# Writing small TensorE operations in the column tiling of the matmuls around them, in a fused audio tower of attention and routed experts

## What is computed

```python
h = _L0_tok_ref(x)                                   # interpolation, 64-point spectra, soft minimum
h = h + _L0_attn_ref(_layernorm(h, axis=-1), ...)    # sigmoid(q k^T * 8) v Wo, relu
h = h + _L0_ffn_ref(_layernorm(h, axis=-1), ...)

# inside the feed-forward layer
all_out = _experts_mlp(x, eW1, eb1, eW2, eb2, eW3, eb3)   # 64 -> 128 -> 64 -> 64, four experts
shared = _shared_mlp(x, sW1, sb1, sW2, sb2, sW3, sb3)     # 64 -> 64 -> 128 -> 64
gates = jax.nn.softmax(x @ gW + gb, axis=-1)
topv, topi = jax.lax.top_k(gates, 2)
topw = jax.nn.softmax(topv, axis=-1)
```

## Time and profile before

| | |
|---|---|
| median of 3 runs | 159.5 us (158.09 to 161.44) |
| the profiled execution | 159.61 us |
| its span, first to last instruction | 157.8 us |
| mean granted TensorE clock | 0.978 |
| TensorE matmul busy | 146.2 us, 93% of the span |
| ScalarE busy | 119.1 us, 75% |
| VectorE busy | 110.8 us, 70% |
| GpSimd busy | 55.3 us, 35% |

### The profile page before, as it was taken

The page is one execution under the profiler, slowest core; times in us unless marked ns, Lnnn a source line. Parts: engine busy times, 40 slices in busy tenths (PEclk is TensorE's granted clock), DMA queues, the critical chain, the costliest instruction groups (busy, mean ns, idle before and its releaser), DMA issues.

```text
span 157.8 us, 6710 instructions
## 1 busy us (share of the span) xinstructions
PE 146.2 (93%) x2856; PEld 87.5 (55%) x2856; DVE 110.8 (70%) x281; ACT 119.1 (75%) x163; POOL 55.3 (35%) x102
## 2 busy tenths in 40 slices
PE   7999686999997999999999999999999999999980
PEld 2478432544574666666665656443657567476480
DVE  2497998998877558586863154879488987877760
ACT  3698982887977899999997989779647867758510
POOL 7000019697695834737356225457000000000000
PEclk9999857999999999999999999999999999999999
DMA  4390000276696692777989700110001011010112
GB/s 118 102 258 1 4 0 0 67 181 145 197 255 206 201 229 72 210 215 224 165 250 179 149 4 13 25 37 0 6 4 32 5 36 34 5 32 13 30 35 67
DMA packets 16722, 15.02 MB, mean 95 GB/s; under 512 B 4780, under 2 KB 15952, under 8 KB 16628
## 3 DMA queue, kind: packets, MB, share of 16 engines
q1 hardware_dynamic: 15924, 13.99, 35.0%
q10 hardware_dynamic: 768, 0.59, 1.3%
HBM read 9.06 MB, written 4.60 MB: 87 GB/s over the span
## 4 chain that ended last, share of the span: by engine, by line
PE 75%; ACT 7%; DVE 7%; POOL 4%; issue 2%; DMA 2%; DVEq 0%; POOLq 0%
PE ps L503 16%; PE ps L485 16%; PE ps L616 9%; PE ps L632 9%; PE ps L514 5%; PE ps L674 4%; PE ps L642 3%; PE ps L696 2%; PE ps L717 2%; DMA area<-x_in 2%; PE ps L540 2%; ACT area L1244 2%; PE ps L444 2%; PE ps L476 1%; ACT square L1242 1%
## 5 line engine op out<-in xcount | busy, mean ns | idle before, releaser
L1309 ACT ACTIVATE probs<-ps 125x1000 f32<-125x1000 f32 x64 | 63.0, 1005 | 8.4 <-PE ps L485 4.1
L503 PE MATMUL ps<-probs,xn 124*32 124x250 f32 (+1 forms) x512 | 40.2, 375 | 0.3 <-ACT probs L1309 0.3
L485 PE MATMUL ps<-YS,XT 128*32 128x500 f16 x448 | 35.9, 375 | 1.0 <-issue 1.0
L1327 ACT ACTIVATE area<-ps,wf 128x500 f32<-128x500 f32 x32 | 21.1, 672 | 7.7 <-PE ps L616 7.7
L936 DVE COPY ZS<-ps 128x250 f32<-128x250 f32 x32 | 13.2, 414 | 17.7 <-PE ps L503 17.7
L503 PEld LDWEIGHTS ps<-probs,xn 124*32 124x32 f32 (+1 forms) x512 | 16.4, 109 | 12.0 <-ACT probs L1309 1.4
L1341 ACT ACTIVATE area<-ps,wf 128x500 f32<-128x500 f32 x20 | 13.5, 676 | 4.7 <-PE ps L642 2.4
L632 PE MATMUL ps<-area,wf 128*64 128x500 f32 x64 | 16.3, 584 | 0.0
L514 PEld LDWEIGHTS ps<-outW,ZS 128*32 128x32 f32 (+1 forms) x512 | 11.7, 108 | 4.8 <-issue 0.9
L485 PEld LDWEIGHTS ps<-YS,XT 128*32 128x32 f16 x448 | 11.2, 96 | 5.6 <-issue 1.7
L514 PE MATMUL ps<-outW,ZS 128*32 128x64 f32 (+1 forms) x512 | 13.1, 219 | 0.2 <-issue 0.2
(11 more groups left out here) (170 smaller groups left out, 260.8 us busy)
## 6 DMA issues: line engine op xcount, KB each, us to landing
YS<-y_stage SPq DMA_DIRECT2D x28, 250.0 KB, 4.1
y_stage<-YP SPq DMA_DIRECT2D x10, 250.0 KB, 3.7
tower_out<-res SPq DMA_DIRECT2D x7, 124.0 KB
wf<-wf_in SPq DMA_DIRECT2D x1, 648.0 KB, 5.8
y_stage<-YP SPq DMA_DIRECT2D x5, 125.0 KB, 3.9
wa<-wa_in SPq DMA_DIRECT2D x1, 512.0 KB, 5.0
y_stage<-YP ACTq DMA_DIRECT2D x3, 125.0 KB, 3.0
ch<-ch_in SPq DMA_DIRECT2D x1, 160.0 KB, 4.8
```

The source lines that it names most:

```text
L485: last = mm(ps[k0:k1, 2 * (n % 2) + j, 0:TG].rearrange("p (h n) -> p h n", h=2), XT[:, g % 3, (2 * bb + cj) * P + k0:(2 * bb + cj) * P + k ...
L503: last = mm(ps[R * hh:R * hh + R, 4 + bb, half * TB:(half + 1) * TB], xn[0:keys, 4 * g + 2 * bb + cj, :], probs[0:keys, n % 3, hh, :], sta ...
L1309: fn(probs[:, n % 3].rearrange("p (j h) n -> p j (h n)", j=2), ps[0:P, 2 * (n % 2):2 * (n % 2) + 2, 0:TG], ACT.Sigmoid, scale=SCORE_SCALE) ...
L1327: fn(H1[:, g % 2, e, :], ps[:, n % 3, 0:TG], ACT.Relu, bias=wf[:, WF["b1"][0] + e:WF["b1"][0] + e + 1]).then_inc(l1_act, 1)
```

## The change

Four operations of TensorE are cut along their output partitions, so that each instruction takes as many columns of the array as the matmuls before and behind it; the first router's logits are spread over more steps, and VectorE reads them later.

- `gates(0, ...)`: each row's matmul becomes four (32, 32, 32 and 29 tokens); two rows instead of four per call, and eight calls instead of four, behind steps 48, 49, 50, 55, 56, 57, 60 and 63.
- `gates(1, ...)`: each row's matmul becomes two (64 and 61 tokens).
- `x2_transpose(7)`: two transpositions of 64 columns per tile instead of four of 32.
- `routing_T(r)`: two transpositions (64 and 8 columns) per row pair instead of one of 72.
- `gate_logits(0)` of VectorE moves behind `add_attention(6)`, `centre2(6)` and `z_take(7, 2)`. Its wait, for as many increments as `GATE_STEPS` has entries, becomes one for eight.

```diff
-GATE_STEPS = tuple(8 * (NG - 2) + t for t in (0, 1, 2, 7))
+GATE_STEPS = tuple(8 * (NG - 2) + t for t in (0, 1, 2, 7, 8, 9, 12, 15))
...
                 for i in range(4):
-                    for c in range(4):
-                        last = nc.tensor.transpose(xt[R * c:R * c + R, i, 0:P], x2s[0:P, g % 2, i, R * c:R * c + R],
+                    for c in range(2):
+                        last = nc.tensor.transpose(xt[F * c:F * c + F, i, 0:P], x2s[0:P, g % 2, i, F * c:F * c + F],
                                                    ident16[0:P, 0:P])
...
                 for i in range(rows.start, rows.stop):
-                    row = NB * r + i
-                    last = mm(ps[0:P, bank, 2 * i * E:2 * (i + 1) * E],
-                              X2T[:, row // 4, row % 4, 0:P],
-                              wg[:].rearrange("p k e -> p (k e)"), start=True, stop=True)
+                    row, wide = NB * r + i, F if r else R
+                    for q0 in range(0, P, wide):
+                        q1 = min(q0 + wide, P)
+                        last = mm(ps[q0:q1, bank, 2 * i * E:2 * (i + 1) * E],
+                                  X2T[:, row // 4, row % 4, q0:q1],
+                                  wg[:].rearrange("p k e -> p (k e)"), start=True, stop=True)
...
                 for b in range(8):
-                    last = nc.tensor.transpose(wt[:, b, 0:P], w16[:, 8 * r + b, :], ident16[0:P, 0:P])
+                    for k0, k1 in ((0, F), (F, KV)):
+                        last = nc.tensor.transpose(wt[k0:k1, b, 0:P], w16[:, 8 * r + b, k0:k1], ident16[0:P, 0:P])
...
-                    gates(0, slice(4 * i, 4 * i + 4))
+                    gates(0, slice(2 * i, 2 * i + 2))
...
                 if g == NG - 1:
-                    gate_logits(0)
                     add_attention(g - 1)
                     centre2(g - 1)
                 z_take(g, 2)
+                if g == NG - 1:
+                    gate_logits(0)
```

## The result

The changed kernel is slower: a median of 161.51 us (six runs, 159.36 to 163.19) against 158.28 us (six runs of the kernel before, 157.9 to 161.44). The ratio is 1.0168, with a 95% interval of 1.0107 to 1.0229; it is formed from the fast executions of either kernel alone, so it lies under the quotient of the two medians. The forecast was 157.2 us, with a range that ended at 159.0. Both the direction and the size were wrong.

What follows compares the result with a forecast made beforehand. TensorE was taken as the bound in nearly every step, down to about 0.90 us. 1.73 - 0.49 + 0.58 + 0.22 + 0.22 = 2.26 us saved, giving 157.2 us on the median of 159.5; range 155.6 to 159.0.

Steps and rivals of the forecast that it cites:

- old logits pieces removed from attention: Attention steps 48 to 50 give up 1.29 us and step 55 0.44 us: 1.73 us saved.
- new ones, seven on the path: Attention: eight narrow matmuls per call, 0.07 us a call, seven calls on the path: 0.49 us added, between 0.21 and 0.78.
- second logits: From line 632 to `layer1`: 1.13 us go, 32 matmuls on 64 columns take 0.55; saved 0.58, between 0.18 and 0.66.
- last token transposition: Line 524 ahead of `layer1`: two gaps of 0.11 us vanish, the four rounds stay; 0.22 us saved.
- routing transposition, r = 1: Line 554, second call: pair of 64 and 8 columns still takes eight rounds, both outer gaps go; 0.22 us saved.
- routing transposition, r = 0: Line 554, first call: both neighbours use 64*64, so the gaps stay; nothing saved.
- VectorE's order: Later `gate_logits(0)` moves the copy behind it to about 100.7, its reader at 101.79; slack 0.6 us, no cost.
- instruction stalls: Rival: 72 more matmuls and as many loads, most between 81 and 99 us, bring another "issue" stall; 158.2 us, chance 0.15.
- dear small matmul: Rival: each of 88 narrow logits matmuls costs 0.058 us, turning point 0.038; 1.8 us slower, 161.3 us; chance 0.04.
- a floor at 0.026: Rival: the 88 logits matmuls' pace has a floor of 0.026 us; saving 1.0 us, 158.5 us; chance 0.08.
- the gaps don't come from the width: Rival: gaps around TensorE's pieces come with the change of operands and all stay; no change, 159.4 us; chance 0.06.
- one more like the larger: Stall rival's size: one further "issue" stall like the 0.98 us at 49.93; saving 1.3 us, 158.2 us; chance 0.15.

Runs made afterwards that it cites:

- the order experiment: Changed kernel with each `routing_T` call's sixteen transpositions reordered, the eight of 64 columns first, then the eight of 8: 158.1 us, ratio 0.9933 to the kernel before.

## Why the prediction was wrong

Step by step, by the profiled executions:

| Step | forecast | measured |
|---|---|---|
| old logits pieces removed from attention | -1.73 | -1.73 (none is left; the size is that read before) |
| new ones, seven on the path | +0.49 | +0.3 (0.04 to 0.05 each) |
| second logits | -0.58 | -0.63 |
| last token transposition | -0.22 | -0.22 |
| routing transposition, r = 1 | -0.22 | +1.88 (2.77 against 0.89) |
| routing transposition, r = 0 | 0 | +2.00 (2.56 against 0.56) |
| VectorE's order | 0 | 0 |
| instruction stalls | a rival | +0.6 on average, not clear of chance |
| sum | -2.26 | +1.6, with the stalls +2.2 |

The ratio of 1.0168 on 158.28 us is 2.7 us (1.7 to 3.6): the sum without the stalls lies just under this interval, the sum with them inside. Between the two profiled executions the sum closes: their spans differ by 159.7 - 157.8 = 1.9 us, and their stalls in attention by 1.7 - 1.5 = 0.2, which leaves 1.7 for the 1.6 of the other rows.

**The step that failed** (term missed: 2.10 + 2.00 = 4.1 us) is the one on the routing weights: "The new pair (64 and 8 columns) lies in different column halves, so again eight rounds: saved 0.22." It asked whether the two pieces lie on different columns, and not whether they have the same tile width. The gap of 0.10 to 0.11 us had been read correctly, and taken as the reason for which the change would help; it was then counted only at the edges of each piece and never inside the one piece that mixes two widths. Fifteen inner gaps and the lost overlap in each of two calls, less one outer gap that the second no longer has, are 3.9 us. The bound "If the halves didn't overlap it would be 16 rounds and 0.25 lost" was too low for the same reason: sixteen rounds with a gap each are 2.56 us, not 0.88. With the step right, the same sum gives -2.26 + 0.22 + 1.88 + 2.00 = +1.84 us, 161.3 on the median of 159.5 and outside the recorded range on the side where the result lies.

The Trainium skill, TensorEngine Tiling (Array Packing), section Tiling Modes, states the rule: a change of tiling mode, not just of tile, drains TensorE. The traces agree, with 0.102 to 0.105 us for a change of width and about as much for a change of rows, and none between tiles of one shape.

**What was right.** The gap comes with a change of width and vanishes with it: lines 524 and 542 have none at their edges now. That it stays where both neighbours use 64*64 was forecast too, without the reason: there it is the rows that change. Narrow matmuls are cheap: 0.016 us each on 64 columns (0.50 / 32; 0.017 forecast), and some 0.005 each on 32 (0.04 / 8). The rivals of the dear small matmul (turning point 0.038) and of a floor at 0.026 fall with that. The Trainium skill, TensorEngine Tiling (Array Packing), section Performance Considerations, has an overhead of some 60 cycles for each matmul. As the pace of the whole engine, 0.025 us by the prediction's estimate, the traces contradict it for tiled matmuls; for a single tile they don't settle it, since two halves side by side take 0.031 us and four quarters add 0.02. The rival by which the gaps don't come from the width falls with the order experiment. The last instruction of `gate_logits(0)` starts at 100.09, and the copy behind it lasts from 100.23 to 100.64, in time for the projection at 101.11; the order cost nothing.

**Half right.** The stall rival named "one more like the larger" for 0.15. In the profiled execution of after it is there (1.08 us), and on average kernels with narrow logits have 0.8 us more near those steps. It was argued from the DMA traffic and the number of instructions only; the blocks of 256 were not seen.

## What to carry to other kernels

Before cutting a TensorE operation for tiling, write down the tile shape, rows and columns, of every instruction in order, its neighbours' included, and count the changes: each costs about 0.10 us here and stops the overlap, and a remainder of 8 columns counts as a width of 32. If a cut leaves a remainder of another width, pad it, use the smaller width for all pieces, or at least issue all pieces of one width together. A gap that argues for a change has to be looked for inside the changed code as well.

## What was not expected of the hardware

- A change of the tile's rows costs as much as one of its columns: 0.10 us between 128*64 and 64*64.
- A TensorE instruction of 8 columns runs beside those of 32 without a gap (24 in 0.54 us) and not beside those of 64 (16 in 2.56 us).
- Eight matmuls that load 32 columns and move 8 add 0.04 us to a stream of 32-column matmuls.
- TensorE can run out of instructions in a fully unrolled kernel: for up to 1.6 us at instruction numbers 193 + 256 k, ending 1.2 to 1.6 us after the block's last packet. These stalls differ between executions, 0 to 3.3 us in all of attention. The five traces of the kernel before have 0 to 2.5 us of them, with spans of 157.1 to 158.8 us; how much of the spread between its runs they make isn't shown.
